# Attention scores from two 64-row halves of queries and keys, three score banks and one bank for turned weights

## The reference

```python
query = seq2 + b_self
key = jnp.concatenate([seq1 + b_prev, seq2 + b_self], 1)
value = jnp.concatenate([seq1, seq2], 1)
q = (query @ Wq + bq).reshape(b, l2, H, DH).transpose(0, 2, 1, 3)
k = (key @ Wk + bk).reshape(b, l1 + l2, H, DH).transpose(0, 2, 1, 3)
v = (value @ Wv + bv).reshape(b, l1 + l2, H, DH).transpose(0, 2, 1, 3)
score_prev = jnp.einsum('bhqd,bhkd->bhqk', q, k[:, :, :l1]) * SCALE
score_self = (q * k[:, :, l1:]).sum(-1, keepdims=True) * SCALE
...
weights = jax.nn.softmax(score, axis=-1)
attn = jnp.einsum('bhqk,bhkd->bhqd', weights[..., :-1], v[:, :, :l1])
attn = attn + weights[..., -1:] * v[:, :, l1:]
return attn @ Wo + bo
```

## Time and profile before

| | us |
|---|---|
| median of 3 runs | 452.03 (449.4 to 454.14) |
| span of the profiled execution | 429.2 |
| PE busy in the span | 375.2 (87%) |
| DVE, ACT, POOL busy | 278.9, 247.4, 197.5 |
| PE's share of the chain that ended last | 58% |
| line 764 (scores), PE busy | 67.8 |
| line 773 (transposes), PE busy | 38.5 |

### The profile page before, as it was taken

The page is one execution under the profiler, slowest core; times in us unless marked ns, Lnnn a source line. Parts: engine busy times, 40 slices in busy tenths (PEclk is TensorE's granted clock), DMA queues, the critical chain, the costliest instruction groups (busy, mean ns, idle before and its releaser), DMA issues.

```text
span 429.2 us, 10202 instructions
## 1 busy us (share of the span) xinstructions
PE 375.2 (87%) x2637; PEld 270.4 (63%) x2637; DVE 278.9 (65%) x1132; ACT 247.4 (58%) x743; POOL 197.5 (46%) x273
## 2 busy tenths in 40 slices
PE   4999999899999995799998998479988779899960
PEld 4456556556666652689998997145565457677650
DVE  4566888888878888376555666369566536365562
ACT  2688788788887891546555564328874124344420
POOL 5421254444334434544554555223737506466561
PEclk9999999999999996599999999569999999899995
DMA  7603999678888404467767675320101122232354
GB/s 150 95 15 97 391 279 251 165 166 199 195 204 182 89 20 136 113 160 180 215 165 199 173 175 155 106 94 21 57 26 52 48 52 72 69 79 76 81 172 147
DMA packets 61072, 57.14 MB, mean 133 GB/s; under 512 B 6042, under 2 KB 49703, under 8 KB 60768
## 3 DMA queue, kind: packets, MB, share of 16 engines
q1 hardware_dynamic: 56288, 48.10, 45.1%
q0 software_dynamic: 4736, 8.47, 5.8%
HBM read 36.12 MB, written 21.73 MB: 135 GB/s over the span
## 4 chain that ended last, share of the span: by engine, by line
PE 58%; issue 12%; DMA 9%; DVE 8%; POOL 6%; ACT 4%; SPq 1%; POOLq 1%; DVEq 0%; ACTq 0%
PE bank L764 13%; PE bank L773 6%; PE bank L896 5%; PE bank L787 5%; PE bank L901 5%; DMA layer_outputs<-w_all 3%; POOL layer_outputs L744 3%; PE bank L1023 3%; DMA w_all<-layer_rows 2%; POOL layer_outputs L702 2%; PE bank L1103 2%; DMA qexp<-layer_outputs 2%; PE bank L804 2%; PE bank L818 2%; PE bank L871 2%
## 5 line engine op out<-in xcount | busy, mean ns | idle before, releaser
L1151 ACT ACTIVATE ps<-bank,ntop 128x128 f32<-128x128 f32 x256 | 73.4, 378 | 11.8 <-DVE ntop L1414 10.1
L1218 ACT ACTIVATE hT<-bank,w 128x128 f32<-128x128 f32 x176 | 50.8, 368 | 40.4 <-PE bank L896 40.1
L764 PE MATMUL bank<-qexp 128*128 128x512 f32 x128 | 67.8, 612 | 0.5 <-ACT ps L1151 0.5
L744 POOL DMA_INDIRECT layer_outputs<-w_all x40 | 39.9, 997 | 39.1 <-DVE w_all L1917 21.7
L773 PEld LDWEIGHTS bank<-ident,ps 128*128 128x128 f32 x256 | 31.9, 141 | 33.3 <-issue 29.8
L896 PE MATMUL bank<-xT,w 128*128 128x128 f32 x352 | 49.1, 284 | 2.8 <-DMA w<-in_L_ffn_w_dram 1.2
L1160 ACT ACTIVATE pT<-bank 128x512 f32<-128x512 f32 x64 | 38.6, 603 | 19.1 <-PE bank L773 18.1
L1413 DVE TENSOR_REDUCE mx<-bank 128x4 f32<-128x512 f32 x64 | 43.7, 683 | 8.5 <-PE bank L764 7.0
L668 POOL TENSOR_TENSOR qexp<-kA,rowmask 128x512 f32<-128x512 f32 x15 | 15.6, 1037 | 69.1 <-DVE kA L1498 69.1
L896 PEld LDWEIGHTS bank<-xT,w 128*128 128x128 f32 x352 | 44.6, 199 | 4.0 <-issue 2.6
L732 POOL DMA_INDIRECT layer_rows<-rows_all,places x32 | 30.8, 961 | 24.7 <-DVE rows_all L1791 10.3
(11 more groups left out here) (328 smaller groups left out, 814.6 us busy)
## 6 DMA issues: line engine op xcount, KB each, us to landing
w<-in_L_ffn_w_dram SPq DMA_DIRECT2D x44, 258.0 KB, 3.4
layer_rows<-fill SPq DMA_DIRECT2D x10, 910.0 KB, 9.1
w_all<-in_L_ffn_w_dram SPq DMA_DIRECT2D x24, 256.0 KB, 4.7
qexp<-layer_outputs SPq DMA_DIRECT2D x8, 512.0 KB, 4.0
xt<-layer_rows SPq DMA_DIRECT2D x45, 65.0 KB
w_all<-layer_rows SPq DMA_DIRECT2D x40, 65.0 KB, 1.9
xfT<-in_xfT_dram SPq DMA_DIRECT2D x16, 128.0 KB, 2.4
layer_rows<-fill SPq DMA_DIRECT2D x1, 1560.0 KB, 12.3
```

The costliest lines, as they stand in the source:

```text
L744: g.indirect_dma_start(ys1_dram, bass.IndirectOffsetOnAxis(ap=xt1[r][:, P:P + 1].bitcast(U32), axis=0), yb1[r][:, :], None, bounds_check=Y ...
L764: pe.matmul(psA[g % 2][:, :], qexp[b % 2][:, g, :], kexp[b % 2].rearrange("p g k -> p (g k)"), start=True, stop=True).then_inc(a_in_ps, 1)
L1151: m = s.activation(ps[g % 2][:, t, :], psA[g % 2][:, t * P:(t + 1) * P], ACT.Exp, bias=ntop[:, h:h + 1])
L1218: s.activation(hT[r % 2][:, c, :], banks[c][:, 0:P], ACT.Gelu, bias=w1[r][:, F0 + c:F0 + c + 1]).then_inc(gelu_done, 1)
```

## The change

The keys are expanded to two copies and no longer to four: `kexp[:, n, :]` keeps the rows of group `n` and of group `n + 2`, so that the upper and the lower 64 rows each hold one group. Each score matmul then takes only 64 rows of queries and of keys and has 256 columns, which are two heads. `scores(b, pair)` replaces `scores(b, g)`: four matmuls, in the order half 0, half 1, half 0, half 1, of which half 0 writes one bank and half 1 another, so that one call fills the banks of two groups. There are two calls in a step, in parts 1 and 3, where there were four.

Three banks now serve the scores, in rotation, and a single one the transposes: T of a group waits for K of the group right before it. The order of heads within the groups changes with it, and the weights are laid out for that. The expansion of the keys writes 256 columns in place of 512, with a mask `halfmask` that one more small DVE operation makes at the start.

```diff
-        kexp = [t[:, 3 * NJ:4 * NJ, :] for t in qexp]
+        kexp = [t[:, 3 * NJ:3 * NJ + NG // 2, :] for t in qexp]
...
-        psT = banks[0:2]
-        psA = banks[2:4]
+        psT = banks[0]
+        psA = banks[1:4]
...
+        def score_bank(b, g):
+
+            return psA[(NG * b + g) % 3]
...
-                    g.tensor_tensor(kexp[b % 2], kA[:, :].unsqueeze(1).broadcast_to([P, NG, P]),
-                                    rowmask[:, :].unsqueeze(2).broadcast_to([P, NG, P]), ALU.mult).then_inc(kexp_ready, 1)
+                    g.tensor_tensor(kexp[b % 2], kA[:, :].unsqueeze(1).broadcast_to([P, NG // 2, P]),
+                                    halfmask[:, :].unsqueeze(2).broadcast_to([P, NG // 2, P]), ALU.mult).then_inc(kexp_ready, 1)
...
-            def scores(b, g):
+            def scores(b, pair):
...
-                atleast(pe, exp_done, 4 * b + (g - 1))
-                pe.matmul(psA[g % 2][:, :], qexp[b % 2][:, g, :], kexp[b % 2].rearrange("p g k -> p (g k)"), start=True, stop=True).then_inc(a_in_ps, 1)
+                atleast(pe, exp_done, 4 * b + (2 * pair - 1))
+                for j in range(2):
+                    for half in range(2):
+                        at = slice(half * (P // 2), (half + 1) * (P // 2))
+                        m = pe.matmul(score_bank(b, 2 * pair + half)[:, 2 * P * j:2 * P * (j + 1)], qexp[b % 2][at, 2 * pair + j, :],
+                                      kexp[b % 2][at, :, :].rearrange("p g k -> p (g k)"), start=True, stop=True)
+                        if j == 1:
+                            m.then_inc(a_in_ps, 1)
...
-                atleast(pe, pT_ready, 4 * b + (g - 1))
+                atleast(pe, pT_ready, 4 * b + g)
...
-                scores(i - 2, 1)
...
-                scores(i - 2, 2)
+                scores(i - 2, 1)
...
-                scores(i - 2, 3)
```

More of the change, by code:

```diff
@@ L428, in attention_moe_kernel @@
         ALL_CONSTS = CONSTS + 32
-        KEYS_MASKED, HEADS_MASKED = 3, 6
+        KEYS_MASKED, HEADS_MASKED = 3, 7
         STEPS = B + 6
@@ L754, in _ @@
             mm_.then_inc(cb_in_ps, 1)
-            def scores(b, g):
+            def scores(b, pair):
                 if not 0 <= b < B:
                     return
-                if g == 0:
+                if pair == 0:
                     pe.wait_ge(qexp_pool, b + 1)
                     pe.wait_ge(kexp_ready, b + 1)
-                atleast(pe, exp_done, 4 * b + (g - 1))
-                pe.matmul(psA[g % 2][:, :], qexp[b % 2][:, g, :], kexp[b % 2].rearrange("p g k -> p (g k)"), start=True, stop=True).then_inc(a_in_ps, 1)
+                atleast(pe, exp_done, 4 * b + (2 * pair - 1))
[6 more added lines that the diff above has]
+                            m.then_inc(a_in_ps, 1)
             def turned_weights(b, g):
@@ L770, in turned_weights @@
                 pe.wait_ge(exp_done, 4 * b + (g + 1))
-                atleast(pe, pT_ready, 4 * b + (g - 1))
+                atleast(pe, pT_ready, 4 * b + g)
                 for j in range(NJ):
-                    m = pe.transpose(psT[g % 2][:, j * P:(j + 1) * P], ps[g % 2][:, j, :], ident[:, :])
+                    m = pe.transpose(psT[:, j * P:(j + 1) * P], ps[g % 2][:, j, :], ident[:, :])
                 m.then_inc(pT_in_ps, 1)
@@ L1150, in weights @@
                     h = place(g, t)
-                    m = s.activation(ps[g % 2][:, t, :], psA[g % 2][:, t * P:(t + 1) * P], ACT.Exp, bias=ntop[:, h:h + 1])
+                    m = s.activation(ps[g % 2][:, t, :], score_bank(b, g)[:, t * P:(t + 1) * P], ACT.Exp, bias=ntop[:, h:h + 1])
                 m.then_inc(exp_done, 1)
@@ L1159, in keep_turned @@
                 atleast(act, pv_done, 4 * b + (g - 1))
-                s.activation(pT[g % 2][:, :], psT[g % 2][:, :], ACT.Identity).then_inc(pT_ready, 1)
+                s.activation(pT[g % 2][:, :], psT[:, :], ACT.Identity).then_inc(pT_ready, 1)
             for i in range(1, STEPS):
@@ L1370, in _ @@
             cc.link(v.tensor_reduce(rowmask[:, :], ind[:, :].rearrange("p (g j) -> p g j", g=NG), AX_X, ALU.add))
-            v.tensor_scalar(rowmask[:, :], rowmask[:, :], 0.0, None, ALU.is_gt).then_inc(rows_masked, 1)
+            cc.link(v.tensor_tensor(halfmask[:, :], rowmask[:, 0:NG // 2], rowmask[:, NG // 2:], ALU.add))
+            v.tensor_scalar(halfmask[:, :], halfmask[:, :], 0.0, None, ALU.is_gt).then_inc(rows_masked, 1)
             def valid_keys(b):
@@ L1407, in below_maximum @@
                 ofg = lambda t: t[:, :].rearrange("p (a t o) -> p a o t", a=2, t=NG)[:, g // 2, g % 2, :]
-                view = psA[g % 2][:, :].rearrange("p (t k) -> p t k", t=NG)
+                view = score_bank(b, g)[:, :].rearrange("p (t k) -> p t k", t=NG)
                 if g == 0:
@@ L1525, in _ @@
                     dve.wait_ge(kA_ready, 1)
-                    v.tensor_tensor(kexp[0], kA[:, :].unsqueeze(1).broadcast_to([P, NG, P]),
-                                    rowmask[:, :].unsqueeze(2).broadcast_to([P, NG, P]), ALU.mult).then_inc(kexp_ready, 1)
+                    v.tensor_tensor(kexp[0], kA[:, :].unsqueeze(1).broadcast_to([P, NG // 2, P]),
+                                    halfmask[:, :].unsqueeze(2).broadcast_to([P, NG // 2, P]), ALU.mult).then_inc(kexp_ready, 1)
                 below_maximum(i - 2, 2)
@@ L1953 @@
     every = lambda name: _np.broadcast_to(laid[name].reshape(1, -1), (P, laid[name].size))
-    grouped = lambda w: w.reshape(-1, NG, 2, 2, DH).transpose(0, 2, 1, 3, 4).reshape(-1, P)
+    grouped = lambda w: w.reshape(-1, 2, 2, NJ, DH).transpose(0, 3, 2, 1, 4).reshape(-1, P)
     laid["xfT"] = _np.concatenate([laid["x"].transpose(0, 2, 1), laid["fside_BxSxS_0"].transpose(0, 2, 1)], axis=2)
```

3 lines of the change are left out of this document (2 added, 1 removed).

## The result

The changed kernel takes 459.78 us (median of 20 runs, 455.14 to 467.07), the one before 453.73 (20 runs, 448.97 to 456.17). The ratio is **1.0121**, with a 95% interval from 1.0097 to 1.0145: slower by 5.5 us. (The medians lie 6.05 apart; the ratio leaves out the runs of either kernel that took over 1.5% longer than its fastest.) The forecast was 452.2 with a range up to 459.0. Of the 7.6 us by which the measured time lies above the forecast, 1.7 belong to the kernel before, whose median was 452.03 when the prediction was made and is 453.73 over 20 runs.

A forecast was written before the change was run, and what follows sets the result against it. PE's work was taken to bound the kernel at 9.36 us a step. Fourteen steps at +0.04 gave +0.6, edges -0.2 and step 8 -0.2: +0.2 us, hence 452.2 us, range 445 to 459.

The forecast's parts named there:

- So E0 starts at S + 1.12 = 2.37 ... so DVE is not late: ACT's first exponentials start 2.37 us after the first pair, behind a copy; DVE's `ntop` is ready at about 2.1.
- the walk: Sum of one attention step, from the first pair's start to the next one's: 9.40 us against 9.36 before.
- E0 to the second pair: From ACT's first exponentials by the values' copy, query projection and keys to the second pair's start: 2.71 us.
- pair to T0: One pair of scores: 0.85 us for halves side by side plus 0.20 at each end for changing mode, 1.25 us.
- T0 to T1: Second transposes wait for the first group's copy out of the single bank: 1.46 us, including 0.22 from release to first pass.
- the fourth rival: The walk is off by an unseen or overcounted wait, over 0.3 us a step; chance 0.08 slower, 0.06 faster.
- The median shown lies 22.8 above that span, with the same work around it: Measured median of before exceeds its traced span of 429.2 us by 22.8, taken as unchanged work around the span.
- The first steps lose about 0.2: At the start of the attention, fewer other matmuls cover the copies of turned weights: about 0.2 us lost.
- The sign that the prediction gave for a wrong assumption: PE's clock falling below 1.00 in the new waits would refute that a pass stays at 0.107 us.
- Step 8: Attention step with extra DVE work, which costs a wait of 1.43 us before: some 0.2 us less.
- The second rival: Two passes of one score matmul hold up the other half: pair 1.46 us, step 9.82, 458.5 us; chance 0.17.
- The two new waits: PE waits twice a step, for the values' copy ahead of the query projection and for the single bank; eats 0.92 us saved.

The follow-up runs named there:

- e1: Changed kernel, with POOL waiting for the maximum of the first group before its sends, so they stand between the pairs: 456.29 us, ratio 1.0021.
- e16: e8 with ten added matmuls whose result nobody reads, to keep PE busy: 446.70 us beside 455.70 for the kernel before, ratio 0.9856.
- e8: Changed kernel, with POOL's sends waiting for `mid_in_ps` of the step before and the queries' projection behind the second pair: 443.83 us beside 446.78, ratio 0.9933.
- e14: Changed kernel with ten added matmuls whose result nobody reads, to keep PE busy in the first steps: 457.77 us, ratio 1.0104.
- e2: Changed kernel, with POOL's sends waiting for the maximum of group 1, to fall beside the second pair: 462.68 us, one run.
- e4: Changed kernel's order and banks, but each group's scores by one matmul of whole rows and 512 columns, keys in four copies: 467.02 us, ratio 1.0286.
- e7: Changed kernel with a pair's four matmuls in the order half 0, half 0, half 1, half 1: 449.69 us beside 446.78.
- e6: Changed kernel with 2 to 16 tiny memsets on POOL ahead of the sends of steps 8 to 15: 446.83 us, one run, beside 446.78 for before.

## Why the prediction was wrong, by its own steps

**The step that failed** is "So E0 starts at S + 1.12 = 2.37 ... so DVE is not late". DVE's `ntop` was to be there at about 2.1 us after S0 and came at 2.98, since DVE learnt of the pair 0.94 us late. (K2' was late too: it began 2.19 us after S0 where 1.89 was forecast, by the late transposes.) Here is the walk against the timeline of the changed kernel, and of e1, where the first pair and the transposes behind it are on time:

| | predicted | e1 | changed |
|---|---|---|---|
| S0 to E0 | 2.37 | 2.25 | 3.01 |
| E0 to the second pair | 2.71 | 2.80 | 2.81 |
| pair to T0 | 1.25 | 1.06 | 1.06 |
| T0 to T1 | 1.46 | 1.44 | 1.44 |
| T1 to the next S0 | 1.61 | 1.73 | 1.73 |
| step | 9.40 | 9.28 | 10.05 |

(e1: 110.43, 112.68, 115.48, 116.54, 117.98, 119.71; changed: 87.83, 90.84, 93.65, 94.71, 96.15, 97.88.) Of the 0.77 between the last two columns 0.76 lie in the first line. The walk took the end of a matmul for the moment at which others see it. Beside an indirect DMA of POOL that is false by up to 1 us, and the change moved the end of the first pair into this place. Before, the late completions in the attention were those that no idle DVE or ACT waited for. It is the fourth rival, a wait that the walk did not see, to which the prediction gave 0.08.

**Behind it stands a misread number**: "The median shown lies 22.8 above that span, with the same work around it". Nothing around the span takes that long; it is 1.8, and the table ahead of the prediction has the same 23 us wrong. The trace came from an execution without late completions, 18.3 us shorter than the next one, 16.9 of them in the second layer. The number did no harm to the sum, which rests on the measured median. The trace alone could not show the lateness, but this gap was the sign that it did not stand for the runs that were timed.

**The first steps lose about 0.2**: mis-sized. They lost 1.4 and 2.2. The prediction took the clock from the steady steps (1.00) and not from the lengths of the passes in the first 20 us. That the start is PE at 1.2 GHz for longer, together with bare waits, is what the lengths of the passes say, and it fits e16, whose passes are fast from the first pair on and whose start is 5.1 us shorter than e8's. e14 shows that filling gaps alone does not give it back. How much of the 1.4 and 2.2 each of the two costs is not separated. The sign that the prediction gave for a wrong assumption, the clock falling in the new waits, came in e1, e2 and e14 and not in the steady steps of the changed kernel.

**Step 8** was to cost 0.2 less with DVE's extra work and cost 1.1 less: 10.19 against the usual 10.05 in place of 10.61 against 9.36. That is a term mis-sized, in the kernel's favour. The wait of 0.22 from a release to the first pass is 0.24 by the rows that it names.

**What held.** The pair costs 1.2 (forecast 1.25), by e4, and the change of mode is paid: in the trace the second pass of a half starts 0.32 us behind the first and the others 0.216 apart, so 0.10 go to weights not loaded ahead, and the transposes start 1.06 behind the pair's start, 0.09 after the last passes have streamed. The second rival did not come: the halves run side by side in either order (e7), and no overlap is missing. The two new waits are where they were said to be, ahead of L828 and of the second transposes, and 1.44 for the single bank was forecast as 1.46. DVE and ACT fit. The last two steps are 13.53 in place of 13.98, the forecast gain of 0.4. The keys' expansion takes 0.61 on POOL (0.52 forecast, 1.03 before). Without the late pair the steps would have been 9.28, 0.08 below before: the balance that the forecast described, gain eaten by waits, is right for the usual steps.

**Open.** Why completions are held beside POOL's indirect DMAs, and why one execution had none of it, no run here tells. (That trace also holds 8267 records of semaphore changes, the second one of the same kernel 5526, so it may have been taken in another way.) Which phase between a send and a completion is hit is known only from examples (e2, e6, e7). Why e1's ratio (1.0 us above before) is some 4 us better than its trace, whose attention is 5.1 us longer, is open too; the traced execution, of 460.99 us, lies 4.7 above the median of its runs, and its start may have been longer than theirs.

## What to carry over

Before resting a walk on a trace, compare its span with the times of the runs: a gap of 5% was here the only sign that the traced execution was not like the ones being timed. Where semaphores are on the path, look for GpSimd's indirect DMAs beside them, and put there only completions that nobody waits for. Taking work from a saturated TensorE paid here only once the order had been rebuilt around the waits which that work had covered (e8, e16), and the first steps, where there is no other work to cover them, must be costed apart.

## What the runs showed of the hardware

- What ends on PE within about 0.65 us of the end of one of GpSimd's indirect DMA instructions is often reported late, by up to 1.5 us where an engine waited for it: 66 of 251 such completions in the second trace of before, 75 of 246 in the changed kernel's. Completions of VectorE and ScalarE there are on time (0 of 308 and 0 of 265). All traces but one show it.
- VectorE's `ntop` (128x4) took 1.61 us beside GpSimd's expansions in e2, and 0.71 in the kernel before, in place of 0.16.
- Two 64-row halves of the array start their passes side by side (7 ns apart in the changed kernel, 14 in e7) whichever half stands first in the queue. The Trainium skill (TensorE: Matmul & The Clock Gate, Part 3) calls the order "strict FIFO"; for starts in different halves the trace of e7 does not agree, and by that rule e7's steps would have been 10.6 in place of 9.3.
- The granted clock read 1.00 in the first 18 to 27 us, where the passes were as long (a pair of halves 2.08 us) as in e1 at a granted clock of 0.50.
